# Sorting graph edges on one core: one load for three index rows, eight load slots, one-hots between product and sum

## What is computed

```python
qkv = x @ qkv_w + qkv_b                      # q, k: 4 heads of 8; v: 4 heads of 16
qe = q[s] * 8 ** -0.5 + edge_attr @ q_rpe_w + q_rpe_b
ke = k[t] + edge_attr @ k_rpe_w + k_rpe_b
ve = v[t] + edge_attr @ v_rpe_w + v_rpe_b
compat = einsum('ehd,ehd->eh', qe, ke)
attn = softmax of compat over the edges with the same s
out = segment_sum(ve * attn, s)
x = layernorm(x + out)
```

## Time and profile before

| what | value |
|---|---|
| median of three runs | 6712.76 us |
| the profiled execution's own time | 6723.71 us |
| its span | 6722.0 us |
| TensorE clock granted, mean of the span | 0.701 |
| busy: PE, DVE, ACT, POOL | 54%, 69%, 46%, 53% |
| sort stage: first to last load issue (L519) | 424.4 to 5808.3 us |

### The profile page before, as it was taken

One profiled execution on the slowest core, in us unless ns is written; L12 is line 12 of the kernel. 1 busy time (PEld: TensorE's weight loads), 2 busy tenths in 40 slices (PEclk: granted clock), 3 DMA queues, 4 the chain that ended last, 5 costly groups with the idle time before them and its releaser, 6 DMA issues. The chain is left out here.

```text
span 6722.0 us, 113212 instructions
## 1 busy us (share of the span) xinstructions
PE 3642.7 (54%) x22344; PEld 3336.9 (50%) x22344; DVE 4669.1 (69%) x18275; ACT 3058.9 (46%) x7584; POOL 3596.2 (53%) x4030
## 2 busy tenths in 40 slices
PE   4654555545545555554555555545455554386786
PEld 3544445444445444444445454445454444365665
DVE  7986666666666666666666666666666666598998
ACT  5964444444444444444444444444444444322332
POOL 0025555555555555555555555555555555565664
PEclk8976665666666666666666666666666666698999
DMA  2013333333333333333333333333333333497897
GB/s 74 19 48 93 95 94 95 98 95 96 97 96 95 97 96 95 94 97 95 98 96 96 94 96 97 93 95 98 92 96 95 96 96 94 133 374 305 339 367 269
DMA packets 628039, 821.65 MB, mean 122 GB/s; under 512 B 216092, under 2 KB 561885, under 8 KB 615007
## 3 DMA queue, kind: packets, MB, share of 16 engines
q1 hardware_dynamic: 510185, 373.02, 21.9%
q0 software_dynamic: 117824, 448.32, 18.1%
HBM read 644.87 MB, written 176.01 MB: 122 GB/s over the span
## 5 line engine op out<-in xcount | busy, mean ns | idle before, releaser
L542 POOL DMA_INDIRECT rec_dram<-recs,place_i x3232 | 3093.7, 957 | 2751.9 <-DVE recs L596 1828.1
L630 PE MATMUL ps_cnt<-hi_hot,lo_hot 128*128 128x98 bf16 x3232 | 371.1, 259 | 2563.8 <-ACT free_rec L691 1615.5
L674 ACT ACTIVATE lo_hotT<-lo_b,minus_p 128x512 f32<-128x512 bf16 x808 | 582.9, 721 | 2585.8 <-DMA w_in<-kv_dram 2300.2
L573 DVE SCALAR_TENSOR_TENSOR matches<-src_b,src_f,ps_const 128x128 bf16<-128x128 int16 (+3 forms) x3232 | 1582.3, 543 | 67.7 <-issue 52.5
L630 PEld LDWEIGHTS ps_cnt<-hi_hot,lo_hot 128*128 128x128 bf16 x3232 | 239.0, 120 | 2730.4 <-issue 2420.5
L639 PE MATMUL ps_look<-free_rec,lo_hotT 128*128 128x98 f32 x6464 | 1408.2, 389 | 2.9 <-ACT lo_hotT L680 2.9
L656 PE MATMUL ps_feat<-w_in,edge_in 115*128 115x128 f32 x6464 | 1348.3, 375 | 44.8 <-issue 44.5
L582 DVE CUSTOM_DVE_ANT_0 picked<-hi_hot,ps_look 128x98 f32<-128x98 bf16 x3232 | 642.3, 252 | 1015.2 <-remote 803.0
L639 PEld LDWEIGHTS ps_look<-free_rec,lo_hotT 128*128 128x128 f32 x6464 | 1286.1, 294 | 3.1 <-ACT lo_hotT L680 3.1
L656 PEld LDWEIGHTS ps_feat<-w_in,edge_in 115*128 115x128 f32 x6464 | 1247.9, 286 | 43.6 <-issue 43.4
L962 PE MATMUL ps_sum<-msg,ident 128*128 128x256 f32 x2744 | 624.5, 386 | 237.7 <-DVE msg L1176 237.7
(11 more groups left out here) (152 smaller groups left out, 3419.1 us busy)
## 6 DMA issues: line engine op xcount, KB each, us to landing
lo_b<-lo_dram SPq DMA_DIRECT2D x808, 128.0 KB
src_b<-src_dram SPq DMA_DIRECT2D x808, 128.0 KB
dst_b<-dl_dram SPq DMA_DIRECT2D x808, 96.0 KB
rec_dram<-recs,place_i POOLq DMA_INDIRECT x3232
edge_in<-in_attr SPq DMA_DIRECT2D x808, 36.0 KB
w_in<-kv_dram SPq DMA_DIRECT2D x808, 36.0 KB
kv_dram<-kvt SPq DMA_DIRECT2D x14, 336.0 KB, 2.7
xt<-in_xT SPq DMA_DIRECT2D x14, 224.0 KB, 3.3
```

Of the source, the lines that this page charges most:

```text
L542: pool.indirect_dma_start(rec_dram[:, :], bass.IndirectOffsetOnAxis(place_i[j][:, m:m + 1], 0), recs[j][:, m, :], None).then_inc(scattered ...
L573: last = dve.scalar_tensor_tensor(matches[j][:, m, 0:before], src_b[j][:, 0:before], src_f[:, bass.ds(u * CT + m, 1)], ps_const[:, CT - m: ...
L630: last = nc.tensor.matmul(ps_cnt[:, 0:NB], lo_hot[j][:, m, :], hi_hot[j][:, m, :], start=False, stop=False, skip_group_check=True)
L674: act.activation(lo_hotT[j][:, :], lo_b[j][:, :], ACT.Abs, bias=minus_p[:, 0:1]).then_inc(lo_off, 1)
```

## The change

One DRAM table `id_dram` of (808, 3, 512) int16 takes the place of the three. One DMA of 3 KB to each of 128 partitions loads digits, sources and targets together, so SP issues three DMAs for a chunk where it issued five. The tiles that loads fill (`edge_in`, `w_in`, `ids_b`) and the records have NU = 8 slots; the other tiles keep NS = 4. The hardware loops' bodies hold eight chunks. On DVE `dots` is split in two: `place` (places and product) comes before the one-hots of the chunk ahead and `total` (the sum) behind them, ahead of the ranks. The slots' constants are set by POOL (slots 1 to 7) and DVE (slot 0), and SP waits for each slot alone.

```diff
-NU = 4
+NU = 8
+NS = 4
...
-    lo_dram = nc.dram_tensor("lo_dram", (NCH, CE), BF16, kind="Internal").ap()
-    src_dram = nc.dram_tensor("src_dram", (NCH, CE), I16, kind="Internal").ap()
-    dl_dram = nc.dram_tensor("dl_dram", (NCH, CE), BF16, kind="Internal").ap()
+    id_dram = nc.dram_tensor("id_dram", (NCH, 3, CE), I16, kind="Internal").ap()
...
-            dve.wait_ge(srcl_in, 16)
-            step(dve.tensor_single_scalar(dig_i[:, :], srcl_i[:, :], P - 1, ALU.bitwise_and))
-            dve.tensor_copy(lo_lin[:, :], dig_i[:, :]).then_inc(lo_made, 1)
-            dve.tensor_copy(src_lin16[:, :], srcl_i[:, :]).then_inc(lo_made, 1)
+            dve.wait_ge(srcl_in, 32)
+            dve.wait_ge(loc_made, WG)
+            step(dve.tensor_single_scalar(dst_l[:, :, :], srcl_i[:, :, :], P - 1, ALU.bitwise_and))
+            dve.tensor_copy(lo_lin[:, :, :], dst_l[:, :, :]).then_inc(lo_made, 1)
+            dve.tensor_copy(src_lin16[:, :, :], srcl_i[:, :, :]).then_inc(lo_made, 1)
...
-        LOADS = {False: 16 * 5, True: 16 * 3}
+        LOADS = {False: 16 * 3, True: 16 * 2}
...
-                if not starts(u, NU):
+                if starts(u, NU):
+                    sp.wait_ge(slots_set[j], 2)
+                else:
                     sp.wait_ge(ranked, u - NU + 1)
                     sp.wait_ge(feats, u - NU + 1)
...
-                sp.dma_start(lo_b[j][:, :], spread(lo_dram, u, P)).then_inc(loaded[j], 16)
-                sp.dma_start(src_b[j][:, :], spread(src_dram, u, P)).then_inc(loaded[j], 16)
+                sp.dma_start(ids_b[j][:, :, :], id_dram[at_u, :, :].partition_broadcast(P).rearrange("p a k e -> p (a k) e")).then_inc(loaded[j], 16)
                 if not general:
-                    sp.dma_start(dst_b[j][:, :], spread(dl_dram, u, WIN)).then_inc(loaded[j], 16)
...
-            def dots(u, j):
+            def place(u, j):
...
+            def total(u, j):
                 dve.wait_ge(dotted, u + 1)
...
+                if not starts(u, 2):
+                    place(u - 2, before)
                 if not ends(u, 1):
                     at_dst(u + 1, ahead)
                     hots(u + 1, ahead)
+                if not starts(u, 2):
+                    total(u - 2, before)
+                if not ends(u, 1):
                     ranks(u + 1, ahead, ahead_turn)
-                if not starts(u, 2):
-                    dots(u - 2, before)
...
+            for c in range(1, NU):
+                pool.memset(edge_in[c][WIN:P, :], 1.0).then_inc(slots_set[c], 1)
+                pool.wait_ge(slots_set[c], 1)
+                pool.tensor_copy(w_in[c][:, :], w_attr[:, :]).then_inc(slots_set[c], 1)
+                pool.wait_ge(slots_set[c], 2)
```

More of the change, by code:

```diff
@@ L144, in tables_stage @@
         xt = [sb(f"xt{i}", [DIM + 1, XG * P]) for i in range(2)]
-        kvt = [sb(f"kvt{i}", [P, XG, KV]) for i in range(2)]
+        spare = T["y"][:, :, :].rearrange("p b f -> p (b f)")
+        kvt = [spare[:, i * XG * KV:(i + 1) * XG * KV].rearrange("p (b f) -> p b f", b=XG) for i in range(2)]
         tail = sb("tail", [S0 + SX, REC])
@@ L180, in _ @@
                 sp.dma_start(xt[i][0:DIM, :], xT[:, i * XG * P:(i + 1) * XG * P]).then_inc(x_in[i], 16)
[L181 to L184, removed]
+            for linear, rows, arrived in ((dst_lin, dst_l, dst_in), (src_lin, srcl_i, srcl_in)):
+                linear = linear.rearrange("(p g e) -> p g e", p=WP, g=WG)
+                for p0, p1 in ((0, WP // 32 * 32), (WP // 32 * 32, WP)):
+                    sp.dma_start(rows[p0:p1, :, :], linear[p0:p1, :, :]).then_inc(arrived, 16)
             sp.wait_ge(w_zero, 1)
@@ L471, in sort_stage @@
         ps_cnt = pb("ps_cnt", [P, 512])
-        ps_feat = [pb(f"ps_feat{c}", [P, CT, FEAT]) for c in range(NU)]
+        ps_feat = [pb(f"ps_feat{c}", [P, CT, FEAT]) for c in range(NS)]
         ps_look = [pb(f"ps_look{i}", [P, CT, P]) for i in range(2)]
-        slots_set, dst_in = sem("slots_set"), sem("sort_dst_in")
+        slots_set, dst_in = [sem(f"slot_set{c}") for c in range(NU)], sem("sort_dst_in")
+        biases = sem("biases")
         const_in, consts_up = sem("const_in"), sem("consts_up")
@@ L546, in step @@
                 if general:
+                    if not starts(u, NS):
+                        pool.wait_ge(feats, u - NS + 1)
                     gather(u, j, turn)
@@ L621, in vector_loop @@
             for u in range(NCH - 2, NCH):
-                dots(u, u % NU)
+                place(u, u % NU)
+                total(u, u % NU)
         def tensor_loop(pe, general):
@@ L629, in step @@
                 for m in range(CT):
-                    last = nc.tensor.matmul(ps_cnt[:, 0:NB], lo_hot[j][:, m, :], hi_hot[j][:, m, :], start=False, stop=False,
+                    last = nc.tensor.matmul(ps_cnt[:, 0:NB], lo_hot[j % NS][:, m, :], hi_hot[j % NS][:, m, :], start=False, stop=False,
                                             skip_group_check=True)
@@ L646, in step @@
                     pe.wait_ge(dst_hotT_made, u + 1)
-                if not starts(u, NU):
-                    pe.wait_ge(dotted, u - NU + 1)
+                if not starts(u, NS):
+                    pe.wait_ge(dotted, u - NS + 1)
                 for m in range(CT):
@@ L651, in step @@
                     if general:
-                        nc.tensor.matmul(ps_feat[j][:, m, :], edge_in[j][WIN:K_ROWS, tile], w_in[j][WIN:K_ROWS, :],
+                        nc.tensor.matmul(ps_feat[j % NS][:, m, :], edge_in[j][WIN:K_ROWS, tile], w_in[j][WIN:K_ROWS, :],
                                          start=True, stop=False)
-                        last = nc.tensor.matmul(ps_feat[j][:, m, 0:KV], ident[:, :], kvg[j][:, m, :], start=False, stop=True)
+                        last = nc.tensor.matmul(ps_feat[j % NS][:, m, 0:KV], ident[:, :], kvg[j % NS][:, m, :], start=False, stop=True)
                     else:
-                        last = nc.tensor.matmul(ps_feat[j][:, m, :], edge_in[j][0:K_ROWS, tile], w_in[j][0:K_ROWS, :],
+                        last = nc.tensor.matmul(ps_feat[j % NS][:, m, :], edge_in[j][0:K_ROWS, tile], w_in[j][0:K_ROWS, :],
                                                 start=True, stop=True)
@@ L731, in _ @@
         def _(dve):
-            for c in range(NU):
-                dve.memset(edge_in[c][WIN:P, :], 1.0).then_inc(slots_set, 1)
-                dve.tensor_copy(w_in[c][:, :], w_attr[:, :]).then_inc(slots_set, 1)
+            dve.memset(edge_in[0][WIN:P, :], 1.0).then_inc(slots_set[0], 1)
+            dve.tensor_copy(w_in[0][:, :], w_attr[:, :]).then_inc(slots_set[0], 1)
+            dve.tensor_scalar(minus_p[:, :], iota_p[:, :], -1.0, None, ALU.mult).then_inc(biases, 1)
+            dve.memset(one[:, :], 1.0).then_inc(biases, 1)
             dve.tensor_copy(ident_b[:, :], ident[:, :]).then_inc(const_in, 1)
@@ L766, in _ @@
             act.activation(free_rec[0][:, :], base[:, :], ACT.Copy).then_inc(table_ready, 1)
-            act.wait_ge(slots_set, 2 * NU + 2)
+            act.wait_ge(biases, 2)
             both_ways(act, scalar_loop)
-def spread(table, chunk, rows):
-    return table[bass.ds(chunk, 1), :].partition_broadcast(rows).rearrange("p a e -> p (a e)")
 def attend_stage(nc, T, rec_dram, out):
```

72 lines of the change are left out of this document (34 added, 38 removed).

## The result

The changed kernel takes **6525.62 us** (median of 4 runs, 6511.17 to 6541.77) beside 6711.2 us of the kernel before (median of 4, 6689.97 to 6715.67): ratio 0.973, 95% interval 0.9699 to 0.9761. It is faster, by 186 us and not by 663, and ends above the range that was given.

The account below looks back on a forecast made before the run. SP's issuing of five loads, 6.68 us a chunk, was taken to bound the sort. 6723.7 - 663 (fewer loads) - 1.5 (tables stage and start of sort) = 6059 us profiled, 6048 us median; range 5580 to 6450 us.

Parts of the forecast that it names:

- It works through its instructions without a pause: SP's queue in the sort: practically never held up, it needs 6.68 us a chunk for five DMAs.
- Two loads fewer, -0.82 us a chunk: SP in the sort: three DMAs instead of five cut a chunk from 6.68 to 5.86 us, -663 us in all.
- SP stays the last to finish: Sort: SP remains the slowest worker after the change, so running ahead through eight slots was priced at 0.
- 5.1 us a chunk: DVE in the sort: work 4.32 plus 0.80 idle before the sum, below 5.86, so DVE does not become the bound.
- the second rival: Sort: slow state reaches PE, ACT and DVE waits; 6.1 to 6.5 us a chunk, 6446 us; chance 0.20.
- New order on DVE, 0: DVE: one-hots hide 0.3 us a chunk of the sum's wait, off the path while loads are late; priced 0.
- Eight slots, 0: SP's loads: running ahead is worth at most the 113 us SP waited for slots, at least 0; taken as 0.
- a queue in front of the slowest worker gives nothing: SP's loads: the reason given for pricing the eight slots at 0.
- Tables stage, +1.5 us: Stage before the sort: three DVE passes over source indices grow from 3232 to 4096 columns, +1.5 us.
- The doubled loop body fetched again: DVE's hardware loop: instruction fetches on each of 99 turns cost 802 us, ending at about 6850 us; chance 0.05.
- Slow steps stop when scatters stop, in every stretch I read: SP in the sort: slow only while POOL scatters; the argument against POOL becoming the bound.
- POOL as the bound: Sort: SP speeds up more and POOL's scatters decide, 5.3 us a chunk, 5600 us; chance 0.15.

Follow-up runs that it names:

- g2: The changed kernel with five loads a chunk again and stores split into 96 and 5 partitions; with stalls 6563.23 us, ratio 0.9755 to the kernel before.
- e10: The kernel before with only the merged load (four slots, old DVE order) and stores split into 96 and 5 partitions; with stalls 6356.22 us, ratio 0.9455.
- e2: The changed kernel with the merged load taken apart, five loads a chunk; without stalls 5459.88 us, ratio 1.0111 to the kernel before.
- e4: The changed kernel with DVE's old order (places, product and sum behind the ranks); without stalls 5458.78 us, ratio 1.0109 to the kernel before.
- e1: The changed kernel with its three 101-partition stores split into 96 and 5; without stalls 5371.35 us, ratio 0.9948 to the kernel before.
- g1: The kernel before with merged load, new DVE order, four slots and split stores; with stalls 6474.19 us, ratio 0.9629.

## Why the prediction was wrong, point by point

- **"It works through its instructions without a pause"**: right. g2, with five loads and eight slots, has SP without waits and ACT waiting 1323 us for the load.
- **Two loads fewer, -0.82 us a chunk, "SP stays the last to finish"**: the step that failed. The merged load moves SP out of the way, but alone it gives 0.43 us. Past that, the waits sit in the handoffs of PE, ACT and DVE. The sum priced SP's queue as if the rest could run at 5.1 us a chunk whenever its loads were there; the versions with the merged load, in which SP waits for slots, take 6.2 to 6.4. That was the second rival, at 6.1 to 6.5 us a chunk and 6446 us, given 0.20: the sort ran at 6.33. Its hint, DVE's wait of 287.5 us for its own semaphore, was a stall on an engine other than SP. The same view of the kernel before has a longer one, which the prediction left out, with DVE's gaps between ranks below it:

```profile
DVE picked L582 <- remote: 454.8, 106, 9.1
...
DVE matches L573 <- issue: 52.0, 85, 1.3
```

The 5.1 us took DVE's idle time before the sum as its own and not the wait before the picks. With 454.8 / 449 = 1.0 us added it would have been 6.1, an estimate. That it lies near the 6.2 of e10 is no proof: there the picks wait little (109.6 us) and the sum more (427.8). Idle engines were taken for idle for want of loads; at least the gaps with no wait behind them were their own.
- **New order on DVE, 0**: mis-sized. It hides the wait of the sum about as priced, loses more in the wait ahead of the picks, and costs 0.15 us a chunk, some 121 us, beside the merged load.
- **Eight slots, 0, "a queue in front of the slowest worker gives nothing"**: the bound held (at most 113 us), but since SP was not the slowest after the merge, the premise fell. They give about 0.06 us a chunk, some 50 us, beside the merged load and the new order.
- **Tables stage, +1.5 us**: mis-sized, +63. The DVE passes were costed; the stores they feed were not. The 8.53 us behind the one store from 101 partitions of the kernel before were there to be read.
- **The doubled loop body fetched again**: did not happen (39 transfers).
- **"Slow steps stop when scatters stop, in every stretch I read"**: the earlier trace rows itself has a slow gap from 3010.45 to 3011.86 us, after POOL's 3009.8. And in e2 scatters run without any slow step, so scatters alone do not make SP slow. A slip without effect: 6048 less the gain of 477 in place of 663 ends at 6234, not 6236.
- **POOL as the bound**: not here, but it is the bound at 5.05 us a chunk, one scatter behind the other, in every version with all its scatters that ran without stalls. There the change as it stands would be about 1.1% slower, by its stores. That is read from e2 to e4; the changed kernel itself was not run without stalls, nor was e10.

Open: what turns the stalls on at one time and not at another (the kernel doesn't, since the same one shows both), whether it is the number of scatters or their being indirect, why the picks wait longer in the new order, and which chain of handoffs bounds once SP is relieved.

## What to carry to other kernels

When the queue that bounds is relieved, ask what the other engines can do in their present state, not what their busy time adds up to: idle time charged to a late load may hide waits of their own. Read every wait row of each engine, not only the one that fits. Look at the partition count of every store that an edit makes or widens, since one from 101 partitions held the queue behind it for 30 us and one split into 96 and 5 for 2. And where the sequencers' own steps vary, time the pieces of a change on more than one chip, because the bound may be another one there.

## What was not expected of the hardware

- The stalls come and go: one chip ran the same kernel in 5399.25 us and later in 6726.38. With stalls a plain register move of the merged load's line lasts up to 1394 ns (profile after), without them 38 (e1, e2).
- They reach DVE too (gaps of 0.6 to 1.3 us between ranks), and with them come waits that no work released, of ACT up to 14.7 us (g1). With four scatters in 6.2 to 6.7 us they are there; the one execution with a scatter every 4.11 us shows none.
- Moving an operation to hide one wait cost more in the next: 204 us less, 423 us more (e10 to g1).
- Stores of 827 KB (808 x 512 x 2 bytes) from 101 partitions take some 33 us each, 25 GB/s, with 0.07 of the 16 DMA engines busy.
